# GpSimd fetches the scan's output and x of each unit by row index

## The chip, the cores and the metric

The kernel runs on one core of a Trainium2 chip. The metric is the device time of one execution in microseconds (us). TensorE (PE in the rows), VectorE (DVE), ScalarE (ACT) and GpSimd (POOL) compute; SyncE (SP) issues most of the transfers between device memory and the on-chip buffers. Every engine works through its own instructions in order and is held up by semaphores.

## What is computed

A block of a transformer on x of shape (4, 2048, 256), in float32:

```python
mod = (_silu(c) @ wmod)                       # sa, ca, ga, sb, cb, gb per batch
h = _layernorm(x) * (1 + ca) + sa
x = x + ga * attention(h)                     # a delta-rule layer, below
h = _layernorm(x) * (1 + cb) + sb
x = x + gb * experts(h)                       # 16 experts, 4 of them chosen, and a shared one

# attention(h): q, k, v from projections and short causal convolutions, then
delta = delta_rule_scan(q, k, v, beta)        # over chunks, in order of tokens
fs, fl = fir(v, 3 taps), fir(v, 31 taps)
stats = [mean and std per head of fs, fl, delta]
p = softmax(router([h, stats]))               # three weights for each head and token
o = p0 * fs + p1 * fl + p2 * delta + id_scale * v
o = o * rsqrt(mean(o * o) + 1e-5) * o_norm_w
return o @ Wo
```

## The kernel before

The kernel is a chain of stages, each a block of its own on all engines: `setup`, `norm_inputs`, `conv_heads`, `long_filter` (the 31 taps), `chunk_inverses`, `delta_scan`, and `mix_and_experts`. A stage ends with a barrier. The scan writes its output, delta, to device memory (`o_d`, 64 tiles of 128 tokens by 256); the last stage reads it back.

`mix_and_experts` starts some 1112 us into the span and works on 16 units of 512 tokens (`UT`; `J` = 4 tiles of 128 tokens). For each unit there are two pieces of work. The **mix** computes the statistics, the router, the mixture o, the projection with Wo, x + ga * (...), called `x2`, and the second layer norm. The **experts** part multiplies by 20 blocks of weights (4 of the shared expert, then 16 experts), `up` and `down` for each. `units_ahead` sets the order: the mix of unit 0 alone (`front`), then for each unit u a `body` that runs the experts of u and, threaded between its steps, the mix of u+1. The mix is cut into 40 small steps s, of which PE, ACT and DVE each take two after each of the 20 blocks. The loop over the bodies is rolled over the first three batches (four bodies in each turn), and the last four bodies are written out.

The inputs of a mix lie in two sets of buffers, by the parity of the unit: `vf` (v and the short filter), `fl` (the long filter), `dl` (delta), `xx` (x), `hT` (the normed h, transposed). SP loads them in `load(u, g, i)`, L1822 to L1836, eight transfers for a unit: one for `vf`, four for `fl`, one each for `dl`, `xx`, `hT`. SP waits first for `x2_done` of the unit two before, after which nothing reads the old content. All count on one semaphore for each parity, `loaded[i]`. Unit 0's `vf`, `fl` and `dl` are already on the chip, read for the scan stage, and SP loads only its `hT` and `xx`.

POOL's work in a body, in order of its queue (L1876 to L1911):
- `mix(u+1)`: two powers (L1880) that make the standard deviations for the statistics out of the variances that DVE has put into `mx_tmp`; then a product with `ids` (L1887), a product with the softmax weights (L1891), two more powers (L1894, L1896), each after a wait for DVE.
- `finish(u)`: after the last expert of unit u, the product with gb (L1903) and the sum with `x2` (L1906).

So the next instruction of POOL after `finish(u-1)` is the first power of `mix(u+1)` in body u. PE needs the result of both powers at step 8 of the mix, after block 4 of 20: there it waits for `std_done`, transposes the statistics (L1927) and goes on. All that PE has to do after this point, the `down` of block 4 first, stands behind that wait:

```python
if s == 8:
    pe.wait_ge(std_done, u * 2 + 2)
    pe.wait_ge(gexp_done, u + 1)
    for j in range(J):
        ins = pe.transpose(M[0][0:K3 * 2 * H, j * P:(j + 1) * P], st[:, j, :], m.ident[:])
```

DVE's `expert` step (L2316) weights each expert's `down` and adds it to `mx_acc`; it waits for PE.

In `chunk_inverses` POOL clears the semaphores of the early stages (L1118), 54 of them, between its first three loads and its first memset.

Of the kernel before, what the change touches and what calls it, by code (L numbers as in the profile page):

```python
# [10 lines left out]
P = 128  # L11
# [4 lines left out]
J = UT // P  # L16
UB = L // UT
NU = B * UB
# [211 lines left out]
def units_ahead(eng, front, body):  # L230

    front(0, 0)
    with eng.Fori(0, B - 1) as b:
        for g in range(UB):
            body(b * UB + g, g, b * UB + (g + 1))
    for g in range(UB):
        u = (B - 1) * UB + g
        body(u, g, u + 1 if g < UB - 1 else None)
# [502 lines left out]
def long_filter(nc, m, w):  # L741
# [10 lines left out]
    with ExitStack() as ctx:  # L752
# [3 lines left out]
        def sem(name):  # L756
            return ctx.enter_context(nc.semaphore(name))
# [12 lines left out]
        store = [sem(f"fl_store{i}") for i in range(RF)]  # L770
# [902 lines left out]
def mix_and_experts(nc, m, w):  # L1673
# [6 lines left out]
    with ExitStack() as ctx:  # L1680
        def sb(name, shape):
            return ctx.enter_context(nc.sbuf_tensor(name, shape, F32))

        def sem(name):
            return ctx.enter_context(nc.semaphore(name))
# [8 lines left out]
        vf = [m.vf0, m.kqT0[:].rearrange("p b a c -> p b (a c)")]  # L1694
        fl = [m.fl0, sb("mx_fl1", [P, J, D])]
# [99 lines left out]
        store = [sem(f"mx_store{i}") for i in two]  # L1795
        block = ctx.enter_context(nc.Block("mix_and_experts"))

        x_v = w.x.rearrange("b (g j p) d -> (b g) p j d", j=J, p=P)
        out_v = w.out.rearrange("b (g j p) d -> (b g) p j d", j=J, p=P)
# [9 lines left out]
        def _(sp):  # L1809
# [8 lines left out]
            sp.sem_inc(loaded[0], 96)  # L1818
# [5 lines left out]
            def load(u, g, i):  # L1824
                rows = bass.ds(u * J, J)

                sp.wait_ge(x2_done, u * 2 + 2)
                sp.dma_start(vf[i][:], m.vf_d[rows].rearrange("j p c -> p j c")).then_inc(loaded[i], 16)
                fl_b = m.fl_d[:, bass.ds(u // UB, 1)].squeeze(1)
                for j in range(J):  # L1830
                    first = (g * J + j) * P
                    sp.dma_start(fl[i][:, j, :].rearrange("p (y c) -> p y c", c=CF),
                                 fl_b[:, first:first + P, :].rearrange("y p c -> p y c")).then_inc(loaded[i], 16)
                sp.dma_start(dl[i][:], m.o_d[rows].rearrange("j p c -> p j c")).then_inc(loaded[i], 16)
                sp.dma_start(xx[i][:], x_v[bass.ds(u, 1)].squeeze(0)).then_inc(loaded[i], 16)
                sp.dma_start(hT[i][:], m.hT_d[bass.ds(u, 1)].squeeze(0)).then_inc(loaded[i], 16)  # L1836

            sp.dma_start(hT[0][:], m.hT_d[0]).then_inc(loaded[0], 16)
            sp.dma_start(xx[0][:], x_v[0]).then_inc(loaded[0], 16)
# [23 lines left out]
        def _(pool):  # L1863
            n = 0
            pool.memset(gsel[:], 1.0).then_inc(const_done, 1)
# [7 lines left out]
            def mix(u, i):  # L1873
# [10 lines left out]
                if isinstance(u, int) and u == 0:  # L1884
                    pool.wait_ge(loaded[i], (u - i) * 64 + 128)
# [10 lines left out]
                pool.tensor_tensor(rstd[:], mv[:, :, 1], m.half_pow[:, 0:J], ALU.pow).then_inc(rstd_done, 1)  # L1896

# [13 lines left out]
            def body(u, g, nxt):  # L1911
                if nxt is not None:
                    mix(nxt, (g + 1) % 2)
                finish(u, g % 2)

            units_ahead(pool, front, body)

        @block.tensor
        def _(pe):
            def mix(u, i, s):  # L1920
# [8 lines left out]
                if 8 <= s < 12:  # L1929
                    f = s - 8  # L1930
                    if f == 0:
                        pe.wait_ge(loaded[i], (u - i) * 64 + 128)
# [181 lines left out]
        def _(dve):  # L2114
            def mix(u, i, s):
                if s < 2:
# [3 lines left out]
                    if s == 0:  # L2120
                        dve.wait_ge(loaded[i], (u - i) * 64 + 128)
# [230 lines left out]
def build(nc, x, Wq, Wk, Wv, Wb, conv_q, conv_k, conv_v, fir_short, fir_long, alpha_id, Wid, bid, Wr1, br1,  # L2352
# [28 lines left out]
    with ExitStack() as ctx:  # L2381
        def sb(name, shape):
            return ctx.enter_context(nc.sbuf_tensor(name, shape, F32))
        m.ident = sb("ident", [P, P])
# [23 lines left out]
        m.ck = sb("ck", [P, NT * H])  # L2408
        mid = ctx.enter_context(ExitStack())
# [63 lines left out]
```

## Time and profile before

| | |
|---|---|
| median of 2 runs | 2588.45 us (2582.2 to 2594.7) |
| the profiled execution: its span | 2587.5 us |
| PE busy | 2394.4 us, 93% of the span |
| DVE busy | 1655.0 us, 64% |
| ACT busy | 1109.5 us, 43% |
| POOL busy | 616.3 us, 24% |
| mean granted clock of PE | 0.946 of full speed |

A profile row gives an instruction's line, engine and operation, what it writes and reads, how long it took, and how long its engine had been idle before it and for whom it waited. The idle time of an engine that waits for something later in the program costs nothing by itself; what counts is the chain of work that ends last. In the last stage that chain runs through PE's matmuls, with short pieces of DVE and POOL.

### The profile page before, as it was taken

How to read it: one execution, taken by the hardware profiler on the slowest of the kernel's cores; microseconds unless marked ns; L12 is line 12 of the kernel's file. 1: busy time of each engine (PE TensorE's matmuls, PEld its weight loads, DVE VectorE, ACT ScalarE, POOL GpSimd, SP SyncE). 2: the span in 40 equal slices, each digit the busy share in tenths (PEclk: the TensorE clock that was granted, in tenths of full speed). 3: DMA queues.
4: the chain of work that ended last, by engine and by line, in shares of the span. 5: the costliest groups of instructions: out<-in, count | busy, mean ns of one | idle time of the engine just before them, and what ended most of it. 6: DMA issues, size and time to landing. Idle time of an engine off the chain costs nothing.

```text
span 2587.5 us, 41994 instructions
## 1 busy us (share of the span) xinstructions
PE 2394.4 (93%) x14594; PEld 1659.7 (64%) x14594; DVE 1655.0 (64%) x4354; ACT 1109.5 (43%) x2350; POOL 616.3 (24%) x417
## 2 busy tenths in 40 slices
PE   6899997667897999979999999999999999999998
PEld 4466665555676888845666666666666666666665
DVE  4487886449922566525767676667667676766675
ACT  2477876346663222224334424433443344244331
POOL 1145554031101111211312231222123132312210
PEclk9999998787667999989999999999999999999999
DMA  5447556978767767421202210220122022101000
GB/s 166 162 149 219 174 166 192 270 212 203 212 155 223 217 204 225 156 74 49 58 1 58 58 50 9 58 58 13 45 59 58 1 58 58 43 15 58 9 9 8
DMA packets 376312, 272.14 MB, mean 105 GB/s; under 512 B 199714, under 2 KB 333794, under 8 KB 373906
## 3 DMA queue, kind: packets, MB, share of 16 engines
q1 hardware_dynamic: 371474, 243.85, 33.6%
q0 software_dynamic: 4640, 25.73, 2.9%
q8 instruction: 115, 1.88, 0.3%
q14 instruction: 83, 0.68, 0.1%
HBM read 168.60 MB, written 100.93 MB: 104 GB/s over the span
## 4 chain that ended last, share of the span: by engine, by line
PE 43%; DVE 9%; issue 3%; POOL 2%; ACT 0%; DMA 0%; DVEq 0%; SPq 0%; POOLq 0%; ACTq 0%
PE mx_dn L2002 16%; PE mx_up L1988 15%; PE mx_m L1938 4%; DVE mx_acc L2316 4%; PE mx_m L1965 2%; POOL mx_rms L1894 2%; PE mx_m L1942 1%; PE mx_m L1979 1%; DVE hl L2224 1%; DVE mx_st L2214 1%; DVE hl L2199 1%; DVE hl L2188 1%; DVE mx_rms L2193 1%; PE mx_m L1973 1%; PE mx_m L1947 1%
## 5 line engine op out<-in xcount | busy, mean ns | idle before, releaser
L2316 DVE SCALAR_TENSOR_TENSOR mx_acc<-mx_dn,mx_comb,mx_acc 128x256 f32<-128x256 f32 x1024 | 424.3, 478 | 356.6 <-PE mx_dn L2002 352.7
L2002 PE MATMUL mx_dn<-mx_edn,mx_hs 128*128 128x256 f32 x2048 | 487.7, 381 | 0.0
L1988 PE MATMUL mx_up<-mx_h2T,mx_eup 128*128 128x512 f32 x1024 | 484.3, 595 | 0.0
L2002 PEld LDWEIGHTS mx_dn<-mx_edn,mx_hs 128*128 128x128 f32 x2048 | 384.4, 190 | 145.6 <-issue 91.0
L2090 ACT ACTIVATE mx_hs<-mx_up 128x512 f32<-128x512 f32 x320 | 190.8, 596 | 625.8 <-PE mx_up L1988 625.1
L1988 PEld LDWEIGHTS mx_up<-mx_h2T,mx_eup 128*128 128x128 f32 x1024 | 190.9, 190 | 156.1 <-issue 145.2
L675 DVE SCALAR_TENSOR_TENSOR cv_acc<-cv_pre,conv_w,cv_acc 128x512 f32<-128x512 f32 x288 | 215.7, 750 | 78.2 <-ACT cv_acc L597 71.3
L539 PE MATMUL cv_pj<-cv_hT,wqkv 128*128 128x512 f32 x384 | 181.8, 604 | 12.7 <-ACT cv_acc L597 7.7
L713 POOL TENSOR_TENSOR rn<-cv_ss,half_pow 128x8 f32 x64 | 127.5, 1992 | 13.2 <-POOL cv_ss L709 13.2
L1880 POOL TENSOR_TENSOR mx_st<-mx_tmp,root_pow 128x24 f32<-128x24 f32 x30 | 124.6, 4168 | 20.1 <-DVE mx_tmp L2142 20.1
L1938 PE MATMUL mx_m<-mx_hT,wr 128*128 128x512 f32 x256 | 122.2, 601 | 3.3 <-DMA mx_x<-_attn_hidden_states_dram 2.5
L1653 ACT ACTIVATE ds_U<-ds_ups 64x256 f32<-64x256 f32 x64 | 24.1, 377 | 232.2 <-PE ds_ups L1517 232.2
L2002 PEld LDWEIGHTS mx_dn<-mx_sdn,mx_hs 128*128 128x128 f32 x512 | 97.3, 190 | 40.5 <-issue 30.6
L1988 PE MATMUL mx_up<-mx_h2T,mx_sup 128*128 128x512 f32 x256 | 120.7, 605 | 2.0 <-issue 2.0
L2002 PE MATMUL mx_dn<-mx_sdn,mx_hs 128*128 128x256 f32 x512 | 121.0, 379 | 0.0
L539 PEld LDWEIGHTS cv_pj<-cv_hT,wqkv 128*128 128x128 f32 x384 | 67.6, 192 | 73.2 <-issue 54.7
L1150 PE MATMUL ci_gps<-ci_kT 64*128 64x128 f32 x768 | 84.8, 361 | 20.5 <-ACT ci_A L1229 13.2
L1575 DVE TENSOR_TENSOR ds_att<-ds_attps,upper 128x256 f32<-128x256 f32 x128 | 48.4, 420 | 84.5 <-PE ds_attps L1495 82.6
L2090 ACT ACT_TABLE_LOAD x76 | 97.5, 1283 | 7.0 <-issue 3.3
L555 PE MATMUL cv_vfps<-diag_fs,cv_vT 128*128 128x128 f32 x768 | 97.4, 277 | 0.0
L817 PE MATMUL fl_ps<-fl_toep,fl_vc 128*84 128x98 f32 x512 | 51.9, 266 | 44.9 <-DVE fl_vc L861 20.6
L555 PEld LDWEIGHTS cv_vfps<-diag_fs,cv_vT 128*128 128x128 f32 x768 | 91.9, 194 | 0.0
(292 smaller groups left out, 3998.7 us busy)
## 6 DMA issues: line engine op xcount, KB each, us to landing
kqT_d<-cv_kqc SPq DMA_DIRECT2D x16, 1024.0 KB, 8.5
vf_d<-cv_vf SPq DMA_DIRECT2D x16, 1024.0 KB, 5.4
fl_toep<-taps_d SPq DMA_DIRECT2D x32, 392.0 KB, 7.3
ds_kqT<-kqT_d SPq DMA_DIRECT2D x10, 1024.0 KB, 5.9
fl_v<-vf_d SPq DMA_DIRECT2D x8, 1216.0 KB
ci_kT<-kqT_d POOLq DMA_DIRECT2D x19, 512.0 KB, 5.7
fl_d<-fl_out POOLq DMA_DIRECT2D x8, 1029.0 KB, 7.2
xin<-_attn_hidden_states_dram SPq DMA_DIRECT2D x16, 512.0 KB, 4.3
```

The costliest lines, as they stand in the source:

```text
L539: ins = pe.matmul(pj[o % 2][:], m.wqkv[:, k, weight(o) * P:(weight(o) + 1) * P], hT[i][:, k, :], start=(k == 0), stop=(k == KD - 1))
L555: ins = pe.matmul(vf_ps[j % 2][:, D + k * P:D + (k + 1) * P], vT[i][:, k, c0 + t:c0 + t + P], m.diag_fs[:, k, t, :], start=(t == 0), stop= ...
L675: ins = dve.scalar_tensor_tensor(out=acc[o % 3][:], in0=pre[i][:, o, t:t + UT], scalar=m.conv_w[:, weight(o), t:t + 1], in1=acc[o % 3][:], ...
L713: pool.tensor_tensor(m.rn[:, bass.ds(u * (J * 2 * H) + j * 2 * H, 2 * H)], ss[j % 2][:], m.half_pow[:, 0:2 * H], ALU.pow).then_inc(rn_done, 1)
L817: ins = pe.matmul(ps[g % RP][0:NA, c // 4, (c % 4) * WIN:(c % 4 + 1) * WIN], vc[:, g % GH * TC + c, :], m.toep[g % RT][:, c, ::-1], start= ...
L1150: ins = pe.matmul(g_ps[n % 2][h % 2][:, h // 2 * P:(h // 2 + 1) * P], kT[k % KB][r, b, h // 2, :], kT[k % KB][r, b, h // 2, :], start=True ...
L1880: pool.tensor_tensor(std[:, :, 1, :], tmp[:, 2, part].rearrange("p (a h) -> p a h", h=H), m.root_pow[:, part].rearrange("p (a h) -> p a h" ...
L1938: pe.matmul(M[(f + 1) % 2][:], m.wr1[:, k, f * P:(f + 1) * P], hT[i][:, k, :], start=(k == 0), stop=False)
L1988: ins = pe.matmul(up_ps[x % 2][:], lhs, h2T[i][:, k, :], start=(k == 0), stop=(k == KD - 1))
L2002: ins = pe.matmul(dn_ps[(i + n) % 2][:, j, :], hs[x % 4][:, j * P:(j + 1) * P], rhs, start=(x == 0 and j % 2 == 0) or x >= NS, stop=(x >= ...
L2090: act.activation(hs[x % 4][:], up_ps[x % 2][:], ACT.Silu).then_inc(silu_done, 1)
L2316: ins = dve.scalar_tensor_tensor(out=acc[i][:, j, :], in0=dn_ps[(i + n) % 2][:, j, :], scalar=comb[i][:, j, e:e + 1], in1=acc[i][:, j, :], ...
```

## The change

`dl` and `xx` are no longer loaded by SP. POOL makes a table of row numbers once (an iota of 128 x 64, `mx_rows_i`). A new function `fetch(u, i)` copies the four columns of unit u into `rows_u[i]`, waits for its own copy and for `x2_done`, and issues eight indirect transfers: for each of the four tiles one of 128 rows of `o_d` into `dl` and one of 128 rows of x into `xx`, 128 KB each. `fetch(0)` and `fetch(1)` stand ahead of the mix of unit 0; `fetch(u+2)` stands at the start of body u, for u = 0 to 13. The transfers count on new semaphores `rows_in[i]`, for which DVE waits at the start of each mix beside `loaded[i]`, whose counts fall by 32 for each unit. The new semaphores and two older sets are allocated once for the whole kernel instead of within a stage, and the semaphores of `long_filter` join the list that POOL clears in `chunk_inverses`.

```diff
@@ long_filter
-        store = [sem(f"fl_store{i}") for i in range(RF)]
+        store = m.fl_store
+        m.early_sems += [*v_in, mm_done, act_turned, dve_turned, *ev_done, m.v_zero, m.v_first, *m.toep_in]
@@ mix_and_experts
+        rows_i = ctx.enter_context(nc.sbuf_tensor("mx_rows_i", [P, NT], mybir.dt.int32))
+        rows_u = [ctx.enter_context(nc.sbuf_tensor(f"mx_rows_u{i}", [P, J], mybir.dt.int32)) for i in two]
...
+        x_rows = w.x.rearrange("b l d -> (b l) d")
+        o_rows = m.o_d.rearrange("n p d -> (n p) d")
@@ sync
-            sp.sem_inc(loaded[0], 96)
+            sp.sem_inc(loaded[0], 80)
...
-                sp.dma_start(dl[i][:], m.o_d[rows].rearrange("j p c -> p j c")).then_inc(loaded[i], 16)
-                sp.dma_start(xx[i][:], x_v[bass.ds(u, 1)].squeeze(0)).then_inc(loaded[i], 16)
                 sp.dma_start(hT[i][:], m.hT_d[bass.ds(u, 1)].squeeze(0)).then_inc(loaded[i], 16)
 
             sp.dma_start(hT[0][:], m.hT_d[0]).then_inc(loaded[0], 16)
-            sp.dma_start(xx[0][:], x_v[0]).then_inc(loaded[0], 16)
@@ gpsimd
+            pool.iota(rows_i[:], [[P, NT]], base=0, channel_multiplier=1).then_inc(iota_done, 1)
+            pool.wait_ge(iota_done, 1)
...
+            def fetch(u, i):
+
+                pool.tensor_copy(rows_u[i][:], rows_i[:, bass.ds(u * J, J)]).then_inc(rows_done, 1)
+                pool.wait_ge(rows_done, u + 1)
+                pool.wait_ge(x2_done, u * 2 + 2)
+                pool.sem_inc(fetch_go, 1)
+                for j in range(J):
+                    pool.indirect_dma_start(dl[i][:, j, :], None, o_rows, bass.IndirectOffsetOnAxis(rows_u[i][:, j:j + 1], 0))\
+                        .then_inc(rows_in[i], 16)
+                    pool.indirect_dma_start(xx[i][:, j, :], None, x_rows, bass.IndirectOffsetOnAxis(rows_u[i][:, j:j + 1], 0))\
+                        .then_inc(rows_in[i], 16)
+
...
             def body(u, g, nxt):
+                if not isinstance(u, int) or u + 2 < NU:
+                    fetch(u + 2, g % 2)
                 if nxt is not None:
                     mix(nxt, (g + 1) % 2)
                 finish(u, g % 2)
 
+            fetch(0, 0)
+            fetch(1, 1)
             units_ahead(pool, front, body)
@@ tensor, and alike on gpsimd and vector
-                        pe.wait_ge(loaded[i], (u - i) * 64 + 128)
+                        pe.wait_ge(loaded[i], (u - i) * 48 + 96)
@@ vector, first step of a mix
+                        dve.wait_ge(rows_in[i], (u - i) * 64 + 128)
```

On POOL, between the body of one unit and the next within the rolled loop, the queue of the kernel before reads thus; the two rows that write `mx_acc` are `finish(u-1)`, and the rows that write `mx_st` are the two powers at the head of the next mix (an ISA row is a semaphore step or a register load).

```order
L1903 TENSOR_TENSOR mx_acc<-mx_acc,gbB 128x1024
L1906 TENSOR_TENSOR mx_acc<-mx_acc,mx_x 128x1024
L1878 ISA
L1880 TENSOR_TENSOR mx_st<-mx_tmp,root_pow 128x6x4
L1878 REGISTER_ALU
L1880 TENSOR_TENSOR mx_st<-mx_tmp,root_pow 128x6x4
L1887 TENSOR_TENSOR kv<-kqT,mx_ids 128x1024
```

At the same place the queue of the changed kernel reads as follows; `mx_rows_u` holds the row numbers, and three more pairs of the two DMA rows follow where the dots stand, before the powers.

```order
L1920 TENSOR_TENSOR mx_acc<-mx_acc,gbB 128x1024
L1923 TENSOR_TENSOR mx_acc<-mx_acc,mx_x 128x1024
L1905 ISA
L1905 COPY mx_rows_u<-mx_rows_i 128x4
L1906 REGISTER_ALU
L1907 ISA
L1910 DMA mx_dl<-o_d,mx_rows_u 128x256
L1912 DMA mx_x<-in_L_attn_hidden_states_dram,mx_rows_u 128x256
...
L1883 REGISTER_ALU
L1885 TENSOR_TENSOR mx_st<-mx_tmp,root_pow 128x6x4 x2
L1892 TENSOR_TENSOR kv<-kqT,mx_ids 128x1024
```

A copy, a semaphore step and eight transfers now stand between the sum with `x2` and the two powers; nothing else on POOL has moved in the bodies.

On SP, the start of the rolled loop's body in the kernel before, from the last transfer of `fl` on:

```order
L1832 DMA mx_fl<-fl_d 128x8x32
L1834 ISA
L1834 DMA mx_dl<-o_d 128x4x256
L1835 ISA
L1835 DMA mx_x<-in_L_attn_hidden_states_dram 128x4x256
L1836 DMA mx_hT<-hT_d 128x1024
L1843 REGISTER_ALU
L1844 ISA
L1844 DMA out_dram<-mx_acc 128x4x256
```

and the same place in the changed kernel:

```order
L1838 DMA mx_fl<-fl_d 128x8x32
L1840 ISA
L1840 DMA mx_hT<-hT_d 128x1024
L1846 REGISTER_ALU
L1847 ISA
L1847 DMA out_dram<-mx_acc 128x4x256
```

The two direct transfers of 512 KB have left SP's queue, and `hT` and the store of the unit's result have moved up by them.

## Rows read from the trace of the kernel before

**Rows 1.** The page: busy us, share of the span and instructions of each engine

```profile
PE 2394.4 (93%) x14594; PEld 1659.7 (64%) x14594; DVE 1655.0 (64%) x4354; ACT 1109.5 (43%) x2350; POOL 616.3 (24%) x417
```

**Rows 2.** Timeline of POOL at one body's start: start, us, instruction, [idle before <-releaser]

```profile
1445.51 2.36 POOL L1903 TENSOR_TENSOR mx_acc<-mx_acc,gbB 128x1024 f32<-128x1024 f32 x1 [12.00 <-DVE mx_acc L2316]
1447.94 2.34 POOL L1906 TENSOR_TENSOR mx_acc<-mx_acc,mx_x 128x1024 f32<-128x1024 f32 x1
1451.16 8.31 POOL L1880 TENSOR_TENSOR mx_st<-mx_tmp,root_pow 128x24 f32<-128x24 f32 x2 [0.88 <-DVE mx_tmp L2142]
```

**Rows 3.** Timeline of PE around step 8, in the body before and in this

```profile
1371.72 0.60 PE L1927 MATMUL mx_m<-ident,mx_st 128*24 128x128 f32 x4
...
1458.82 1.88 PE L1988 MATMUL mx_up<-mx_h2T,mx_eup 128*128 128x512 f32 x4
1460.54 0.60 PE L1927 MATMUL mx_m<-ident,mx_st 128*24 128x128 f32 x4
1460.97 1.88 PE L1938 MATMUL mx_m<-mx_hT,wr 128*128 128x512 f32 x4
```

**Rows 4.** Timeline of DVE in the same body, the first experts' sums

```profile
1466.56 1.66 DVE L2316 SCALAR_TENSOR_TENSOR mx_acc<-mx_dn,mx_comb,mx_acc 128x256 f32<-128x256 f32 x4 [0.21 <-DVE mx_comb L2300]
...
1472.85 1.66 DVE L2316 SCALAR_TENSOR_TENSOR mx_acc<-mx_dn,mx_comb,mx_acc 128x256 f32<-128x256 f32 x4 [4.34 <-PE mx_dn L2002]
1479.26 1.66 DVE L2316 SCALAR_TENSOR_TENSOR mx_acc<-mx_dn,mx_comb,mx_acc 128x256 f32<-128x256 f32 x4 [4.75 <-PE mx_dn L2002]
```

**Rows 5.** Timelines of POOL and PE in the next body, which opens a loop turn

```profile
1536.76 2.35 POOL L1906 TENSOR_TENSOR mx_acc<-mx_acc,mx_x 128x1024 f32<-128x1024 f32 x1
1541.53 8.30 POOL L1880 TENSOR_TENSOR mx_st<-mx_tmp,root_pow 128x24 f32<-128x24 f32 x2 [2.43 <-DVE mx_tmp L2142]
...
1550.63 0.60 PE L1927 MATMUL mx_m<-ident,mx_st 128*24 128x128 f32 x4
```

**Rows 6.** POOL's instructions grouped: xcount | busy us, mean ns | idle before

```profile
L709 POOL TENSOR_TENSOR cv_ss<-cv_ss,l_eps 128x8 f32<-128x8 f32 x64 | 39.1, 611 | 140.9 <-DVE cv_ss L684 140.9
...
L1896 POOL TENSOR_TENSOR mx_rstd<-mx_mv,half_pow 128x4 f32<-128x4 f32 x16 | 16.1, 1006 | 191.1 <-DVE mx_mv L2220 191.1
...
L1096 POOL DMA_DIRECT2D ci_kT<-kqT_d x19 | 14.3, 755 | 57.7 <-PE ci_gps L1150 50.6 <-POOLq L752 7.0
```

**Rows 7.** The instructions of one line: POOL's stores of `fl_d` (duration ns min/median/max)

```profile
L784 POOL DMA_DIRECT2D fl_d<-fl_out x8: 513/513/755, 461.7 to 536.2; - x8
```

**Rows 8.** Timeline of POOL in `chunk_inverses`: a transfer and the memset behind it

```profile
556.95 0.76 POOL L1096 DMA_DIRECT2D ci_kT<-kqT_d  x1
557.70 0.97 POOL L1124 MEMSET ci_half<- 128x1024 f32 x1
```

**Rows 9.** The instructions of one line: the semaphores cleared there, first and last start

```profile
L1118 POOLq EVENT_SEMAPHORE_RANGE_CLEAR  x54: 44/44/48, 544.5 to 548.3; - x54
```

**Rows 10.** Timelines of PE at the start of the last stage (mix of unit 0)

```profile
1115.78 2.07 PE L2010 MATMUL mx_dn<-wr,ident 128*128 128x512 f32 x2 [4.75 <-DVE mx_pick L2346]
...
1121.20 5.56 PE L1938 MATMUL mx_m<-mx_hT,wr 128*128 128x512 f32 x8 [2.50 <-DMA mx_x<-_attn_hidden_states_dram]
...
1128.59 3.70 PE L1938 MATMUL mx_m<-mx_hT,wr 128*128 128x512 f32 x8 [0.77 <-ACT mx_hm L2054]
```

**Rows 11.** Stretches: us, busy of five engines, granted clock, DMA share, GB/s

```profile
1115.00:1120.00 5.00, 2.93 (x6) 1.07 (x6) 0.23 (x1) 1.23 (x3) 1.25 (x4) 0.50 0.54 169
1120.00:1125.00 5.00, 3.80 (x5) 1.73 (x6) 0.35 (x2) 1.23 (x1) 1.90 (x1) 0.50 0.99 290
1125.00:1130.00 5.00, 4.23 (x12) 1.45 (x12) 0.00 (x0) 1.27 (x2) 0.00 (x0) 1.00 0.83 199
...
1460.00:1480.00 20.00, 20.00 (x65) 10.58 (x64) 10.39 (x24) 12.80 (x15) 1.90 (x1) 1.00 0.22 75
```

**Rows 12.** Timelines of POOL and DVE in the mix of unit 0

```profile
1116.27 0.52 POOL L1870 TENSOR_SCALAR_AFFINE_SELECT mx_esel<-mx_esel 128x256 f32<-128x256 f32 x1
1121.79 1.90 POOL L1887 TENSOR_TENSOR kv<-mx_vf,mx_ids 128x1024 f32<-128x1024 f32 x1 [5.01 <-DVE mx_ids L2149]
1140.91 2.96 POOL L1891 TENSOR_TENSOR kv<-mx_vf,mx_pr 128x1024 f32<-128x1024 f32 x1 [17.21 <-DVE mx_pr L2172]
...
1166.88 1.01 POOL L1896 TENSOR_TENSOR mx_rstd<-mx_mv,half_pow 128x4 f32<-128x4 f32 x1 [12.62 <-DVE mx_mv L2220]
...
1138.88 0.21 DVE L2153 TENSOR_TENSOR mx_pr<-mx_m,rtau 128x48 f32<-128x48 f32 x1 [17.24 <-PE mx_m L1952]
...
1146.24 1.22 DVE L2188 TENSOR_TENSOR hl<-hl,kv 128x1024 f32<-128x1024 f32 x1
```

**Rows 13.** Timeline of PE at step 8 of the mix of unit 1

```profile
1194.08 0.60 PE L1927 MATMUL mx_m<-ident,mx_st 128*24 128x128 f32 x4
```

**Rows 14.** DMA issues: xcount, KB each, median us from issue to landing

```profile
mx_dl<-o_d SPq DMA_DIRECT2D x16, 512.0 KB, 4.5
...
mx_x<-_attn_hidden_states_dram SPq DMA_DIRECT2D x16, 512.0 KB, 5.2
```

More of the change, by code:

```diff
@@ L1794, in mix_and_experts @@
         last_step = sem("mx_last_step")
-        store = [sem(f"mx_store{i}") for i in two]
+        store = m.mx_store
+        iota_done, rows_done, fetch_go, rows_in = m.iota_done, m.rows_done, m.fetch_go, m.rows_in
         block = ctx.enter_context(nc.Block("mix_and_experts"))
         x_v = w.x.rearrange("b (g j p) d -> (b g) p j d", j=J, p=P)
+        x_rows = w.x.rearrange("b l d -> (b l) d")
+        o_rows = m.o_d.rearrange("n p d -> (n p) d")
         out_v = w.out.rearrange("b (g j p) d -> (b g) p j d", j=J, p=P)
@@ L1884, in mix @@
                 if isinstance(u, int) and u == 0:
-                    pool.wait_ge(loaded[i], (u - i) * 64 + 128)
+                    pool.wait_ge(loaded[i], (u - i) * 48 + 96)
                 pool.wait_ge(ids_step, u * 2 + 2)
@@ L2120, in mix @@
                     if s == 0:
-                        dve.wait_ge(loaded[i], (u - i) * 64 + 128)
+                        dve.wait_ge(loaded[i], (u - i) * 48 + 96)
+                        dve.wait_ge(rows_in[i], (u - i) * 64 + 128)
                     if isinstance(u, int) and u == 0:
@@ L2383, in sb @@
             return ctx.enter_context(nc.sbuf_tensor(name, shape, F32))
+        m.mx_store = [ctx.enter_context(nc.semaphore(f"mx_store{i}")) for i in range(2)]
+        m.iota_done = ctx.enter_context(nc.semaphore("mx_iota_done"))
+        m.rows_done = ctx.enter_context(nc.semaphore("mx_rows_done"))
+        m.fetch_go = ctx.enter_context(nc.semaphore("mx_fetch_go"))
+        m.rows_in = [ctx.enter_context(nc.semaphore(f"mx_rows_in{i}")) for i in range(2)]
         m.ident = sb("ident", [P, P])
@@ L2408, in build @@
         m.ck = sb("ck", [P, NT * H])
+        m.fl_store = [ctx.enter_context(nc.semaphore(f"fl_store{i}")) for i in range(3)]
         mid = ctx.enter_context(ExitStack())
```

## Prediction

> **What bounds the kernel now.** I read the busy shares first [rows 1]: PE works 93% of the span, POOL 24%, so PE sets the pace and POOL has room on average. An average says nothing of a deadline inside a unit, so next come the timelines of one body. Each body of the last stage takes 88.8 us (PE's step 8 at 1371.72 and at 1460.54 [rows 3]; 90.1 to the next at 1550.63, which opens a turn of the loop [rows 5]). Within it the reader is to follow POOL from the end of one unit to the start of the next [rows 2]: the sum with x2 ends at 1447.94 + 2.34 = 1450.28, the first power starts 0.88 later, when DVE's variances are there, and the two powers end at 1451.16 + 8.31 = 1459.47. PE starts the transposes that need them at 1460.54 with no idle time shown [rows 3]. So POOL meets PE's deadline by 1460.54 - 1459.47 = 1.07 us, and all that may be put ahead of the powers at no cost is 0.88 + 1.07 = 1.95 us. Where a loop turn opens, the same sum is 1550.63 - (1536.76 + 2.35) - 8.30 = 3.22 us [rows 5].
>
> What if PE is late there? DVE after this point waits for PE: 4.34 and 4.75 us before the second and third expert's sum [rows 4]. It hurries nothing and makes up nothing; its work moves later with PE's. A delay of PE at step 8 is a delay of the unit, whole. PE's clock is also at stake: the stretch around this point is granted 1.00 [rows 11].
>
> **The change, part by part.**
>
> *Eight indirect transfers and a copy ahead of the powers, in bodies 0 to 13.* The trace before has no indirect transfer. POOL's direct ones occupy it: 0.513 us for a store of 84 long rows [rows 7], 0.755 for a load in 512 pieces of 1 KB [rows 6], and the memset behind one starts when it ends, 556.95 + 0.76 against 557.70 [rows 8]. Issuing is thus work that POOL does in line. An indirect transfer of 128 rows writes 128 pieces of 1 KB, so its lower bound is the direct price, 0.51. On top POOL must read 128 row numbers from the chip's buffer. The cheapest of POOL's small operations that read a tile is 0.61 us (L709, 128 x 8), one of the index table's own width 1.01 (L1896, 128 x 4, a power) [rows 6]. The upper bound is 0.755 + 1.01 = 1.76. I take 0.51 + 0.61 = 1.12, because an index read is nearer to a plain read than to a power. Eight are 9.0 us. The copy of 128 x 4 and its two waits: nothing at the least, 0.7 at the most (0.61 by L709 and a semaphore step), I take 0.5. Together 9.5 us a body (bounds 4.4 and 14.8).
>
> The Trainium skill has a rule on this in "DMA: Bandwidth & Descriptors", section "Anatomy of one DMA — SWDGE (gpsimd) path": the fixed 2 us of such a transfer is mostly completion, and generating descriptors is a small, variable part of which one can emit a lot before it shows. The rows agree for direct ones (some 430 pieces more cost 0.24 us); by that rule the sum would be the lower bound's. No row here shows it with an index read.
>
> What stands behind: the two powers on POOL, then PE's transposes, PE's `down` of block 4, and with it DVE and ACT. Delay a body: 9.5 - 1.95 = 7.55 us, and 9.5 - 3.22 = 6.28 where a loop turn opens. Of the 14 bodies, body 0 has more room: POOL is free at 1166.88 + 1.01 = 1167.89 [rows 12] and PE's step 8 is at 1194.08 [rows 13], so 26.19 - 8.30 = 17.9 us are free, and nothing is lost. Of bodies 1 to 13, two (4 and 8) open a loop turn. Sum: 11 x 7.55 + 2 x 6.28 = 95.6 us. Bounds: 11 x 2.45 + 2 x 1.18 = 29 and 11 x 12.85 + 2 x 11.58 = 165.
>
> *PE's clock after such a stall.* At the start of this stage PE idles for 4.75 us, and the granted clock is 0.50, the lower of its two levels (1.2 of 2.4 GHz), over the next 10 us, then 1.00 again [rows 10, 11]. Eight matmuls of L1938 took 5.56 us there and 3.70 after it; the two before took 2.07 instead of 2 x 3.70/8 = 0.93 [rows 10]. Lost: 1.86 + 1.14 = 3.0 us. A stall of 7.5 us a body is longer than that idle time, so I count 3.0 for each of 13: 39 us. Bounds: 0, if the clock stays, and half of ten, 5.1, if the whole 10 us are filled: 0 to 66.
>
> *The transfers themselves.* They land after some 5 us [rows 14], and DVE first needs them a body later, about 88.8 us; even several times that is covered. DVE's new wait for `rows_in` therefore costs nothing in the bodies, and the 16 direct transfers of each array that it replaces were as well covered.
>
> *The mix of unit 0.* Here POOL has to issue 16 transfers ahead of its product L1887. POOL's constants end at 1116.79 [rows 12]; with the iota, no longer than the select of 0.52 there, at 1117.3. `fetch(0)` ends at 1126.8 and lands at 1132.0 with the 5.2 of [rows 14]; DVE waits there, but first has other than the two small `ids` steps to do at 1138.88 [rows 12]: covered. `fetch(1)` ends at 1136.3, L1887 at 1138.2, before L1891 can start at 1140.91: covered. At 1.76 each, `fetch(1)` would end at 1146.9, L1887 and L1891 (1.90 + 2.96) at 1151.8, and DVE's sum that wants them at 1146.24 would be 5.5 late; that is the upper bound. PE gains a little: it waited 2.50 us for x [rows 10], which SP no longer loads; PE now waits for `hT` alone, issued just before. Between 0 and 2.5; I take 0.5.
>
> *22 more semaphores cleared.* 54 took from 544.5 to 548.3 [rows 9], 70 ns each; 22 more are 1.5 us on POOL ahead of its first memset and further loads of `ci_kT`. At worst it comes through whole: +1.5; at best nothing. I take 1.5.
>
> *SP.* Two transfers fewer for each unit; nobody waits for SP's queue in the bodies. Zero.
>
> Sum: 95.6 + 39 - 0.5 + 1.5 = 135.6. On the profiled execution's own span of 2587.5 us that gives 2723 us; the median of the runs, 2588.45, is the same within 0.1%.
>
> **The rivals.**
>
> *Cheap issue: no change to speak of.* POOL writes the 128 pieces almost as fast as a direct transfer, 0.55 us each, and the short stall leaves the clock alone. Then a body has 4.8 us of fetch, the stall is 2.85 us (1.6 at a loop turn), together 35 us: 2587.5 + 35 + 1 = 2623 us. For it: 0.513 in [rows 7]. Against it: the row numbers have to be read, and PE's clock fell after 4.75 us. It holds up to 0.7 us a transfer (13 stalls and 1 us more then come to 2%), and only if the clock stays; if the clock falls each time, 39 us of the 52 are gone, and only a fetch of 3.1 us would do. 0.12.
>
> *Dearer issue, 1.9 to 4 us a transfer.* POOL would wait within each transfer for something that no row shows. At 3 us: fetch 24.5, delay 22.5 x 11 + 21.3 x 2 = 290, clock 39, body 0 late by 6.6, unit 0's mix by some 26 (49 from 1117.3, then 4.86, against 1146.24): 2587.5 + 362 = 2950 us. 0.10.
>
> *POOL becomes the bound.* If each row number is fetched by itself, one after the other, at 611/8 = 76 ns (L709's price for a column [rows 6]), a transfer takes 9.8 us, a fetch 78.7. Delay: 11 x 76.7 + 2 x 75.5 = 995, 133 in unit 0's mix (two fetches from 1117.3 to 1274.7, then 4.86), 61 in body 0, 45 of clock and the rest: 3820 us. For it: no row shows POOL reading one number per partition to address memory. Against it: POOL's 512 pieces in 0.755 us are 1.5 ns each, far from 76. The Trainium skill states such a price in "GPSIMD Engine Reference", section "7. Performance pitfalls for Q7 kernels": about 102 cycles for every small read command, one per gather index, that doesn't overlap the one before; at its 1.2 GHz that is 85 ns, and by it alone the time would be some 3960 us (an estimate). No run here shows it. 0.06.
>
> *Faster.* All that could be gained is PE's 2.50 us at the start of the stage. 0.02 for anything beyond 2%.
>
> **How the numbers follow.** Two per cent is 52 us, about what a measurement of this kernel can tell from no change. My forecast, a transfer of 0.7 to 1.9 us with the clock falling, has 0.70: its bounds are 2587.5 + 29 + 39 at the low end (2655) and 165 + 66 + 5.5 + 1.5 at the high one (2825). The cheap rival (0.12) ends as "same", the two dear ones (0.10, 0.06) as slower, so slower is 0.86, same 0.12, faster 0.02. To leave out no more than 2 in 10 the range goes from 2640, which reaches into the cheap rival's upper end, to 2830; outside remain most of the cheap rival and the dear ones.
>
> **What would show it.** In the profile of the changed kernel: the mean of POOL's DMA rows at L1910 and L1912 (1.1 us forecast); POOL's idle time before L1885 gone, because the powers now start when the fetch ends; PE idle before the transposes of `mx_st` (now L1948) with POOL's L1885 as releaser, 7.5 us in 13 bodies and none in body 0; the granted clock at 0.50 right behind; body length up from 88.8 to about 99.3 us; no wait of DVE for `rows_in` but in unit 0. I am wrong if PE does not wait at L1948, if the DMA rows are under 0.7 us, or if DVE's or PE's time moves elsewhere, for instance by transfers that land later than a body after their issue.

## The result, and the profile after

The changed kernel takes 2748.11 us (2748.07 to 2748.16, 2 runs) against 2588.45 us: a ratio of 1.062, with a 95% interval of 1.056 to 1.068. The profiled execution has a span of 2746.4 us, 158.9 us more than the one before. The forecast was 2723 us, within 2640 to 2830.

The page of the changed kernel, busy time of each engine and, from its fourth part, the chain of work that ended last by engine:

```profile
PE 2435.5 (89%) x14594; PEld 1682.2 (61%) x14594; DVE 1657.0 (60%) x4354; ACT 1111.3 (40%) x2350; POOL 755.6 (28%) x562
...
PE 33%; POOL 11%; DVE 9%; issue 5%; ACT 0%; DVEq 0%; DMA 0%; POOLq 0%; SPq 0%; ACTq 0%
```

The same chain in the kernel before:

```profile
PE 43%; DVE 9%; issue 3%; POOL 2%; ACT 0%; DMA 0%; DVEq 0%; SPq 0%; POOLq 0%; ACTq 0%
```

PE has the same 14594 matmuls as in [rows 1]. POOL has 139 us more of work and is still idle for 72% of the span, but its share of the chain went from 2% to 11%. An engine with ample room on average now sets the end in places. The view of PE's waits says where (waited for, us in total, times, longest):

```profile
PE mx_m L1948 <- POOL mx_st L1885: 127.1, 13, 11.3
```

In the kernel before this wait has no row at all. It is step 8 of the mix, PE waiting for the two powers, 13 times. POOL's timeline at the start of one body shows what stands ahead of them; it answers to [rows 2]:

```profile
1376.81 2.35 POOL L1923 TENSOR_TENSOR mx_acc<-mx_acc,mx_x 128x1024 f32<-128x1024 f32 x1
1379.11 0.18 POOL L1905 COPY mx_rows_u<-mx_rows_i 128x4 int32 x1
1380.19 1.07 POOL L1910 DMA_INDIRECT mx_dl<-o_d,mx_rows_u  x1 [0.90 <-POOL mx_rows_u L1905]
1381.56 0.95 POOL L1912 DMA_INDIRECT mx_x<-_attn_hidden_states_dram,mx_rows_u  x1 [0.30 <-issue]
...
1386.56 1.00 POOL L1912 DMA_INDIRECT mx_x<-_attn_hidden_states_dram,mx_rows_u  x1 [0.30 <-issue]
1387.86 1.68 POOL L1910 DMA_INDIRECT mx_dl<-o_d,mx_rows_u  x1 [0.30 <-issue]
1389.84 0.95 POOL L1912 DMA_INDIRECT mx_x<-_attn_hidden_states_dram,mx_rows_u  x1 [0.30 <-issue]
1390.81 8.51 POOL L1885 TENSOR_TENSOR mx_st<-mx_tmp,root_pow 128x24 f32<-128x24 f32 x2
```

From the end of the sum with x2 (1376.81 + 2.35 = 1379.16) to the first power (1390.81) it is 11.65 us, where there was 0.88 before. Most of the transfers take 0.95 us (the first takes 1.07, the seventh 1.68), and 0.30 us of idle time follows each: 1.25 us from start to start. PE at the same place, against [rows 3]:

```profile
1387.68 1.88 PE L2009 MATMUL mx_up<-mx_h2T,mx_eup 128*128 128x512 f32 x4
1399.45 1.02 PE L1948 MATMUL mx_m<-ident,mx_st 128*24 128x128 f32 x4 [9.88 <-POOL mx_st L1885]
1400.26 2.88 PE L1959 MATMUL mx_m<-mx_hT,wr 128*128 128x512 f32 x4
1402.98 1.89 PE L2023 MATMUL mx_dn<-mx_edn,mx_hs 128*128 128x256 f32 x8
```

PE idles for 9.88 us, and then its first matmuls are slow: 1.02 us for what took 0.60, 2.88 for 1.88. The same stretch cut in windows (us, busy of five engines, granted clock, DMA share, GB/s), against [rows 11]:

```profile
1390.00:1392.00 2.00, 0.00 (x0) 0.00 (x0) 1.97 (x2) 1.11 (x2) 1.98 (x2) 1.00 1.15 308
1392.00:1402.00 10.00, 2.55 (x7) 1.32 (x8) 3.03 (x10) 1.46 (x3) 7.32 (x2) 0.50 0.11 39
1402.00:1412.00 10.00, 10.00 (x32) 5.30 (x31) 1.91 (x6) 5.26 (x6) 1.90 (x1) 0.99 0.01 2
```

The clock falls to its lower level while PE idles, and stays there for some 10 us; PE works for 2.55 of these. DVE makes up nothing. Its timeline behind the stall, against [rows 4]:

```profile
1404.90 1.66 DVE L2338 SCALAR_TENSOR_TENSOR mx_acc<-mx_dn,mx_comb,mx_acc 128x256 f32<-128x256 f32 x4 [9.67 <-PE mx_dn L2023]
...
1413.13 1.66 DVE L2338 SCALAR_TENSOR_TENSOR mx_acc<-mx_dn,mx_comb,mx_acc 128x256 f32<-128x256 f32 x4 [6.28 <-PE mx_dn L2023]
1419.54 1.66 DVE L2338 SCALAR_TENSOR_TENSOR mx_acc<-mx_dn,mx_comb,mx_acc 128x256 f32<-128x256 f32 x4 [4.75 <-PE mx_dn L2023]
```

It waited 0.21 us for `mx_comb` before the first sum and now waits 9.67 us for PE; the third waits 4.75 as before.

Because a run's span also holds what happens in the six earlier stages, the experiments are compared by a distance inside the last stage: from the start of PE's step-8 transposes of unit 1 to that of unit 15, each read from PE's timeline. That is 14 bodies with all 13 stalls. Before, it is 1245.8 us (14 x 88.8 and a little at the loop turns). "Rest" is what the distance has grown by, less the wait.

| kernel | unit 1 to unit 15, us | over before | PE's wait for POOL in it | rest | rest for each of 13 stalls |
|---|---|---|---|---|---|
| after | 1399.7 | 153.9 | 127.1 | 26.8 | 2.1 |
| after, once more (e8) | 1401.9 | 156.1 | 127.5 | 28.6 | 2.2 |
| SP loads, rest kept (e3) | 1245.9 | 0.1 | 0 | 0.1 | |
| fetch behind the powers (e1) | 1247.2 | 1.4 | 0 | 1.4 | |
| x only (e2) | 1329.7 | 83.9 | 57.0 | 26.9 | 2.1 |
| direct on POOL (e4) | 1324.5 | 78.6 | 55.5 | 23.1 | 1.8 |
| sixteen of 64 rows (e7) | 1522.9 | 277.0 | 246.8 | 30.2 | 2.2 (of 14) |
| ten matmuls added (e6) | 1376.8 | 131.0 | 15.8 | 115.2 | 0.1 beside the 8.75 added |
| twenty matmuls added (e5) | 1485.4 | 239.5 | 0 | 239.5 | less than the 17.33 added |

In e7 PE also waits in body 0; that wait lies ahead of the distance, but what follows it lies within, so its rest is shared by 14 stalls.

Of the 158.9 us, 127.1 are PE's waits and 26.8 the rest; the last 5.0 lie outside this distance.

### The profile page after: what moved, and what is told of

Read it like the earlier page. It is cut to its first block, busy times and chain, and to the rows that moved or that the text cites. A ratio compares the mean times of both kernels' runs of the same rounds, so it can differ in the third digit from the quotient of the medians.

```text
span 2746.4 us, 42140 instructions
## 1 busy us (share of the span) xinstructions
PE 2435.5 (89%) x14594; PEld 1682.2 (61%) x14594; DVE 1657.0 (60%) x4354; ACT 1111.3 (40%) x2350; POOL 755.6 (28%) x562
## 3 DMA queue, kind: packets, MB, share of 16 engines
q8 instruction: 115, 1.88, 0.3%
## 4 chain that ended last, share of the span: by engine, by line
PE 33%; POOL 11%; DVE 9%; issue 5%; ACT 0%; DVEq 0%; DMA 0%; POOLq 0%; SPq 0%; ACTq 0%
PE mx_dn L2023 12%; PE mx_up L2009 9%; DVE mx_acc L2338 5%; PE mx_m L1959 5%; POOL mx_st L1885 4%; POOL mx_dl L1910 2%; PE mx_m L1986 2%; POOL mx_x L1912 2%; POOL mx_rms L1899 2%; PE mx_m L1963 1%; POOL mx_acc L1920 1%; PE mx_m L2000 1%; DVE hl L2246 1%; DVE mx_st L2236 1%; DVE hl L2221 1%
## 5 line engine op out<-in xcount | busy, mean ns | idle before, releaser
L2009 PEld LDWEIGHTS mx_up<-mx_h2T,mx_eup 128*128 128x128 f32 x1024 | 190.9, 190 | 156.1 <-issue 145.2
L1959 PE MATMUL mx_m<-mx_hT,wr 128*128 128x512 f32 x256 | 140.1, 677 | 1.7 <-DMA mx_hT<-hT_d 1.0
L713 POOL TENSOR_TENSOR rn<-cv_ss,half_pow 128x8 f32 x64 | 127.5, 1991 | 13.2 <-POOL cv_ss L709 13.2
L1948 PE MATMUL mx_m<-ident,mx_st 128*24 128x128 f32 x64 | 15.6, 395 | 127.1 <-POOL mx_st L1885 127.1
L1885 POOL TENSOR_TENSOR mx_st<-mx_tmp,root_pow 128x24 f32<-128x24 f32 x30 | 127.6, 4261 | 1.2 <-DVE mx_tmp L2164 0.9
L2075 ACT ACTIVATE mx_hm<-mx_m,br 128x512 f32<-128x512 f32 x64 | 43.8, 687 | 133.6 <-PE mx_m L1963 133.2
```

The costliest lines, as they stand in the source:

```text
L713: pool.tensor_tensor(m.rn[:, bass.ds(u * (J * 2 * H) + j * 2 * H, 2 * H)], ss[j % 2][:], m.half_pow[:, 0:2 * H], ALU.pow).then_inc(rn_done, 1)
L1885: pool.tensor_tensor(std[:, :, 1, :], tmp[:, 2, part].rearrange("p (a h) -> p a h", h=H), m.root_pow[:, part].rearrange("p (a h) -> p a h" ...
L1959: pe.matmul(M[(f + 1) % 2][:], m.wr1[:, k, f * P:(f + 1) * P], hT[i][:, k, :], start=(k == 0), stop=False)
L2009: ins = pe.matmul(up_ps[x % 2][:], lhs, h2T[i][:, k, :], start=(k == 0), stop=(k == KD - 1))
```

## The experiments

**Does anything but the transfers cost time?** SP loads both arrays again, while the table, the copy with its wait, the new semaphores and the longer clearing list stay. Left out below are the counts of `loaded`, which go back to the old ones, SP's load of unit 0's x, and DVE's wait for `rows_in`, which goes.

```diff
@@ sync, load
+                sp.dma_start(dl[i][:], m.o_d[rows].rearrange("j p c -> p j c")).then_inc(loaded[i], 16)
+                sp.dma_start(xx[i][:], x_v[bass.ds(u, 1)].squeeze(0)).then_inc(loaded[i], 16)
@@ gpsimd, fetch
-                for j in range(J):
-                    pool.indirect_dma_start(dl[i][:, j, :], None, o_rows, bass.IndirectOffsetOnAxis(rows_u[i][:, j:j + 1], 0))\
-                        .then_inc(rows_in[i], 16)
-                    pool.indirect_dma_start(xx[i][:, j, :], None, x_rows, bass.IndirectOffsetOnAxis(rows_u[i][:, j:j + 1], 0))\
-                        .then_inc(rows_in[i], 16)
```

> No indirect transfer is left: SP loads both arrays directly; POOL still makes its table, copies the columns of each unit, waits and counts, and the semaphores are allocated and cleared as in the changed kernel. Theory A: 0.2 to 1.2 us a body fit into the 1.95 us of room, nothing waits; 2594 us if the later start of the last stage (5.3 us in the profile) comes from the bookkeeping of the semaphores, 2588 us if that was chance.

It took 2584.67 us (2581.05 to 2594.99, 10 runs), ratio 0.998 (0.996 to 1.001), and its bodies are those of before (0.1 us over all of them). So no cost of POOL's bookkeeping shows, nor one of the longer list of semaphores; the interval would hide no more than some 1 us.

**Is it the transfers, or their place?** The same eight transfers, put behind the two powers instead of ahead of them.

```diff
-            def mix(u, i):
+            def mix(u, i, then=None):
@@ mix, behind the second power
+                if then is not None:
+                    then()
@@ body
-                if not isinstance(u, int) or u + 2 < NU:
-                    fetch(u + 2, g % 2)
+                more = not isinstance(u, int) or u + 2 < NU
                 if nxt is not None:
-                    mix(nxt, (g + 1) % 2)
+                    mix(nxt, (g + 1) % 2, (lambda: fetch(u + 2, g % 2)) if more else None)
```

> The eight indirect transfers of each body stay on POOL, but stand behind the two powers instead of ahead of them. Theory A (what costs is the place: the fetch delays the powers, and PE waits for them at step 8): PE's wait at L1948 is gone, the clock stays, the product with ids comes some 2.5 us later on POOL, where it has 20 us to spare; 2594 us, that is before plus the 5 to 6 us by which the last stage already began later in the profile of the changed kernel. Rival B (the indirect transfers cost as such: by their number, by contention for buffers or memory, or by landing late): it stays above 2700 us.

It took 2591.68 us (2586.71 to 2607.7, 10 runs), ratio 1.0025 (1.0002 to 1.0048). POOL's timeline of one body in this kernel:

```profile
1368.50 8.30 POOL L1885 TENSOR_TENSOR mx_st<-mx_tmp,root_pow 128x24 f32<-128x24 f32 x2 [0.88 <-DVE mx_tmp L2165]
1376.75 0.47 POOL L1907 COPY mx_rows_u<-mx_rows_i 128x4 int32 x1
1378.10 1.14 POOL L1912 DMA_INDIRECT mx_dl<-o_d,mx_rows_u  x1 [0.89 <-POOL mx_rows_u L1907]
1379.55 0.95 POOL L1914 DMA_INDIRECT mx_x<-_attn_hidden_states_dram,mx_rows_u  x1 [0.30 <-issue]
...
1387.99 1.92 POOL L1894 TENSOR_TENSOR kv<-kqT,mx_ids 128x1024 f32<-128x1024 f32 x1
```

The copy and the transfers cost POOL about what they did, 11.2 us of a body (1376.75 to 1387.99) against 11.65, and the powers have their 0.88 us back. PE has no wait for them. So the loss is the place in POOL's queue: all of it but some 3 us goes when the fetch stands behind two instructions instead of ahead of them. GpSimd can fetch these rows at next to no cost; it only may not do so ahead of the powers.

**Half the transfers.** POOL fetches x, SP loads delta; the counts that follow from it are left out below.

```diff
@@ sync, load
+                sp.dma_start(dl[i][:], m.o_d[rows].rearrange("j p c -> p j c")).then_inc(loaded[i], 16)
@@ gpsimd, fetch
-                    pool.indirect_dma_start(dl[i][:, j, :], None, o_rows, bass.IndirectOffsetOnAxis(rows_u[i][:, j:j + 1], 0))\
-                        .then_inc(rows_in[i], 16)
```

> POOL fetches x alone (four indirect transfers a body, at the old place); SP loads the scan's output directly as before the change. Theory A: the fetch falls from 11.65 us to 1.07 + 4 x 1.25 = 6.1 us, PE's wait at step 8 from 9.8 to about 4.3 us, the clock still falls in each body (2.4 us): 13 x 6.7 = 87 us and 5 us from the stages ahead, 2680 us. If the price were mostly fixed for a body (the copy, its waits, the clock), it would stay above 2720 us; if the clock fell only behind long stalls, 2650 us.

It took 2668.74 us (2663.7 to 2678.41, 4 runs), ratio 1.034 (1.030 to 1.037). PE's waits:

```profile
PE mx_m L1947 <- POOL mx_st L1886: 57.0, 13, 4.6
```

Four transfers fewer take 70.1 us from the waits, 5.4 for each body: four times 1.25, and the one long transfer, which this kernel doesn't have, less what its powers take more. The price of the fetch grows with the number of transfers. The rest stays at 2.1 us for each stall, though the stall is less than half as long.

**What does the row index cost?** The same eight transfers of 128 rows, in the same place, as direct ones without an index tile; `x_t` is x seen as tiles of 128 rows.

```diff
-                    pool.indirect_dma_start(dl[i][:, j, :], None, o_rows, bass.IndirectOffsetOnAxis(rows_u[i][:, j:j + 1], 0))\
-                        .then_inc(rows_in[i], 16)
-                    pool.indirect_dma_start(xx[i][:, j, :], None, x_rows, bass.IndirectOffsetOnAxis(rows_u[i][:, j:j + 1], 0))\
-                        .then_inc(rows_in[i], 16)
+                    pool.dma_start(dl[i][:, j, :], m.o_d[bass.ds(u * J + j, 1)].squeeze(0)).then_inc(rows_in[i], 16)
+                    pool.dma_start(xx[i][:, j, :], x_t[bass.ds(u * J + j, 1)].squeeze(0)).then_inc(rows_in[i], 16)
```

> POOL issues eight direct transfers of 128 rows at the place of the eight indirect ones, of the same rows and sizes; the table and the copy stay. If reading the row numbers is what makes an indirect transfer dearer than the 0.51 us of a direct one (0.95 us busy was measured), a transfer falls to 0.51 us busy plus 0.30 between two, the fetch to some 8.3 us, the delay to 6.3: 13 x 8.7 = 113 us over 2590, 2703 us. If writing 128 pieces costs the same either way, 2748 us.

It took 2664.57 us (2651.09 to 2679.56, 4 runs), ratio 1.028 (1.023 to 1.033), some 40 us less than expected. POOL's timeline, and PE's row behind it:

```profile
1384.46 0.54 POOL L1912 DMA_DIRECT2D mx_x<-_attn_hidden_states_dram  x1
1385.01 9.39 POOL L1886 TENSOR_TENSOR mx_st<-mx_tmp,root_pow 128x24 f32<-128x24 f32 x2
...
1394.53 1.03 PE L1947 MATMUL mx_m<-ident,mx_st 128*24 128x128 f32 x4 [4.49 <-POOL mx_st L1886]
```

Direct transfers follow one another at 0.54 us without a gap, near the 0.51 of [rows 7]; indirect ones at 1.25. The index tile therefore makes a transfer 0.71 us dearer, and eight are 5.7 us. With the one long transfer of each body gone (0.7 more), PE's wait should fall by 6.4; it fell by 5.4 in this body, since the powers now take 9.39 us instead of 8.51 (more on that below).

**By the transfer or by the row?** Sixteen indirect transfers of 64 rows in place of eight of 128.

```diff
-            pool.iota(rows_i[:], [[P, NT]], base=0, channel_multiplier=1).then_inc(iota_done, 1)
+            pool.iota(rows_i[:], [[64, 2 * NT]], base=0, channel_multiplier=1).then_inc(iota_done, 1)
...
-                for j in range(J):
-                    pool.indirect_dma_start(dl[i][:, j, :], None, o_rows, bass.IndirectOffsetOnAxis(rows_u[i][:, j:j + 1], 0))\
+                for j in range(2 * J):
+                    r = slice(j % 2 * 64, j % 2 * 64 + 64)
+                    pool.indirect_dma_start(dl[i][r, j // 2, :], None, o_rows, bass.IndirectOffsetOnAxis(rows_u[i][0:64, j:j + 1], 0))\
...
```

> The same rows in sixteen indirect transfers of 64 rows a body in place of eight of 128. If an indirect transfer's price is mostly fixed, each stays near 0.95 us busy plus 0.30: the fetch is 21.9 us, 13 x 22.3 us of delay and clock, and the mix of unit 0 starts some 18 us late: about 2900 us. If it is mostly by the row, each falls to some 0.5 us, the fetch is 14.3 us: about 2785 us.

It took 2886.09 us (2881.49 to 2894.16, 4 runs), ratio 1.116 (1.111 to 1.120), near the number for a fixed price. The instructions of the line that fetches delta (duration ns min/median/max), first of this kernel, then of the changed one:

```profile
L1911 POOL DMA_INDIRECT mx_dl<-o_d,mx_rows_u x128: 902/907/1667, 1118.9 to 2636.8; - x128
```

```profile
L1910 POOL DMA_INDIRECT mx_dl<-o_d,mx_rows_u x64: 942/946/1696, 1123.6 to 2497.0; - x64
```

Half the rows take 0.04 us from the median, with the same 0.30 us gap behind. The price is per transfer. The row numbers are not paid for one by one: 64 of them cost 0.04 us, where the rival that forecast 3820 us wanted 76 ns each. The Trainium skill's "GPSIMD Engine Reference", section "7. Performance pitfalls for Q7 kernels", puts a price of about 102 cycles on each of many small read commands, such as one for each index; the trace does not agree for this instruction, and the measurement decides.

This kernel also shows where the cover of body 0 ends. PE's wait for the powers comes 14 times, once more than elsewhere, and the additional one is 5.2 us, in body 0: a fetch there lasts 21.5 us (16 x 1.21, 1.08 for the copy, and a long one), and the room, 17.9 us in the prediction, is 16.4 here (POOL is free at 1185.02, and without its wait PE would be there at 1209.75; the powers take 8.34).

**Is the rest the clock?** If PE works ahead of step 8 instead of idling, the wait is filled and the clock should stay. Twenty matmuls whose result nobody reads are added there, in every body.

```diff
                 if s == 8:
-                    pe.wait_ge(std_done, u * 2 + 2)
                     pe.wait_ge(gexp_done, u + 1)
+                    if not isinstance(u, int) or u > 0:
+                        for y in range(20):
+                            pe.matmul(M[0][:], m.ident[:], m.wr1[:, y % KD, :], start=True, stop=True)
+                    pe.wait_ge(std_done, u * 2 + 2)
```

> The changed kernel with twenty matmuls of 128 x 512 that nothing reads (9.3 us at the full clock) put on PE ahead of its wait at step 8 in each body, so that PE is busy while POOL fetches. If the clock's fall behind the stall costs what the profile seems to show (each body is some 12 us longer, but PE's wait is 9.8), the granted clock stays at 1.00 and the time falls by 13 x 2.4 = 31 us to 2717 us. If those 2.4 us are something else, it stays at 2748 us or rises.

It took 2849.57 us (2846.23 to 2857.27, 4 runs), ratio 1.103 (1.099 to 1.107): a miss, and one of the filler's size. PE's timeline:

```profile
1411.95 17.33 PE L1948 MATMUL mx_m<-wr,ident 128*128 128x512 f32 x40
1429.11 0.60 PE L1951 MATMUL mx_m<-ident,mx_st 128*24 128x128 f32 x4
```

Each of the twenty stands as two matmuls, so that they take 17.33 us and not some 9; they outlast the wait, and PE waits no more for POOL. The transposes take 0.60 us again. But with the filler longer than the wait, the time alone can't tell how the clock counts, so the next run has ten at the same place, in the bodies up to the one that holds the mix of unit 14.

```diff
+                    if not isinstance(u, int) or 0 < u < NU - 1:
+                        for y in range(10):
+                            pe.matmul(M[0][:], m.ident[:], m.wr1[:, y % KD, :], start=True, stop=True)
```

> As the run with twenty unread matmuls on PE ahead of its wait at step 8, but with ten. Its trace showed each of them as two passes of 0.433 us, 17.3 us in place of the 9.3 counted, so they outlasted the fetch; ten are 8.7 us and end before the powers do (PE waited 9.8 us). If the clock's fall costs 2.4 us a body, 13 bodies give back 31 us and body 0, where PE did not wait, loses 8.7: 22 us less than the changed kernel, 2726 us. If the clock is not it, 2757 us.

It took 2735.95 us (2725.99 to 2738.18, 4 runs), ratio 1.056 (1.052 to 1.061). The changed kernel beside it on the same chip:

> The changed kernel unaltered, beside the next three on one chip. 2748 us, within 10 us to either side, since the kernel before scatters by that much from run to run.

2744.9 us (2742.56 to 2748.59, 4 runs), ratio 1.061 (1.057 to 1.065). PE does more work and ends 9 us earlier. That is less than expected, and the intervals of the two ratios overlap, so the bodies must decide. PE's timeline with ten matmuls added, and its granted clock there:

```profile
1396.65 8.75 PE L1948 MATMUL mx_m<-wr,ident 128*128 128x512 f32 x20
1406.62 0.61 PE L1951 MATMUL mx_m<-ident,mx_st 128*24 128x128 f32 x4 [1.23 <-POOL mx_st L1885]
1407.06 1.88 PE L1962 MATMUL mx_m<-mx_hT,wr 128*128 128x512 f32 x4
```

```profile
1405.00:1410.00 5.00, 3.77 (x15) 2.25 (x15) 0.00 (x0) 2.46 (x3) 1.56 (x1) 1.00 0.00 0
```

8.75 us of filler and 1.23 of wait hold PE as long as the 9.88 of the changed kernel did, the clock stays at 1.00 (it falls in one body only, behind a wait of 2.69 us), and most bodies take 98.8 us, where the changed kernel's take 100.1 to 102.7. In the table the rest falls from 2.1 us for a stall to 0.1. So the rest is the clock, and it is worth 2 us a stall.

## Why the prediction was right, and by how much its terms were off

**The place of the loss: right.** A room of 1.95 us in front of a deadline of PE; PE late by what the fetch exceeds it; the unit later, whole. The wait sits at L1948 with L1885 as releaser, in bodies 1 to 13 and not in body 0, and at the two loop turns it is 8.57 and 8.39 us instead of 9.88, lower by 1.3 to 1.5 where the prediction had 1.27. In body 12, the first that is written out, it is 11.31, which the prediction hadn't singled out. Moving the fetch by two places in the queue undoes it (e1).

**The price of a transfer: 1.12 forecast, 1.25 measured.** The busy part, 0.95, was too dear in the forecast and the gap of 0.30 behind it wasn't in it. The step was "0.51 + 0.61", the direct price and the cheapest small read; the direct price holds (0.54 in e4), and the index adds 0.71. The copy and its waits were put at 0.5; copy and wait take 0.18 + 0.90 = 1.08, since POOL idles until its own copy is signalled. And one transfer a body takes 1.41 to 1.96 us instead of 0.95. A fetch is then 11.65 us, not 9.5. Less 1.95 of room, plus the 0.20 us by which the powers got longer (8.51 against 8.31), that is the 9.88 us that PE waits. Term: 95.6 forecast, 127.1 measured. (The lower bound of 4.4 us for a fetch is eight times 0.55; with the 0.51 named there it is 4.1, and the term's lower bound 25 us instead of 29. The 26 us of the dearer rival in unit 0's mix come to 24.9. Neither moves the range.)

**The clock: 3.0 forecast, 2.1 measured for a stall.** The 3.0 came from the start of the stage [rows 10, 11], where PE works through most of its 10 slow us. Here the low clock begins within the stall, so part of it falls on time in which PE does nothing anyway: in the windows above PE works 2.55 of 10 us at 0.50, half of which, 1.3 us, is lost; that body is 100.2 us against the 98.8 with the clock kept. Of the other eleven bodies between two stalls four take 100.1 to 100.3 as well, the rest 100.9 to 102.7; in the one of 101.5 PE works 5.02 of the 10 us at 0.50 (1293 to 1303). Term: 39 forecast, 26.8 measured. The two errors have opposite signs, and their sum, 134.6 against 153.9, leaves 19.3 us that the forecast missed within the bodies; that the total came nearer than its largest term, which was 31.5 us short, is luck.

**What was put at nothing.** The bookkeeping on POOL: 0.1 us over all bodies (e3). Body 0: no wait. SP's shorter queue: nobody waited for it. DVE waits for a fetched row just once, in the mix of unit 0, as forecast (15.6 us, where it has little else to do); transfers land in 5.5 us at the median, a body ahead of need. Unit 0's mix: from its transposes to those of unit 1 it is 75.9 us, 76.4 before, and 68 to 76 in the profiles of e1 to e4 (e7, with twice the transfers, has 96.6), so no loss shows, and a gain as small as the 0.5 forecast can't be read. Within it one piece of work got slower: POOL's product L1892, now behind both fetches, runs beside DVE's L2191, which takes 1.87 us there and 0.21 in the other 15 mixes. PE's wait for x of 2.50 us [rows 10] is one of 1.0 for `hT`.

**The semaphores: 1.5 forecast, nothing found.** 76 clears now run where 54 did:

```profile
L1119 POOLq EVENT_SEMAPHORE_RANGE_CLEAR  x76: 37/38/47, 543.8 to 548.6; - x76
```

From the first start to the last it is 4.8 us where [rows 9] had 3.8, the last starts 0.3 us later, and e3, which has them all, is not slower. The 5.0 us outside the distance come from the start of the last stage, where POOL's first instruction is at 1120.99 instead of 1115.46. This start moves from run to run, from 1116 to 1135 us by the first transposes in these profiles, in no relation to the edits; runs of one kernel differ by some 20 us. Nothing here ties it to the change.

**The rivals.** "Cheap issue" (0.55 us a transfer, clock untouched, 2623 us) would have been near for direct transfers: e4 has that price, but the clock falls there too, behind 11 of its 13 waits (4.49 us in most bodies), and it takes 2665. "Dearer issue" falls with 1.25 us, "POOL becomes the bound" with e7, and nothing became faster. None of these kernels beats the one before; e1 comes within 0.5% of it.

## What to carry to other kernels

Before work is put on an engine that looks idle, find the next instruction behind it for which another engine waits, and the slack of that one; here it was 2 us in a body in which POOL worked a quarter of the time, and two places further down the queue there was room for all of it. An indirect transfer's price on POOL is by the transfer, so move many rows with each. And a stall of the matrix engine costs more than its length: add what the clock gives away behind it, about 2 us on average for stalls of 4 to 19 us here.

## What the runs showed of the hardware that was not expected

**An indirect transfer keeps POOL for 1.2 us or a little more, with 64 rows as with 128:** 0.95 busy and a gap of 0.30 for 128 rows of 1 KB, 0.91 and 0.30 for 64 rows, against 0.54 without a gap for a direct one.

**Beside some operations of DVE it takes longer, by a simple sum.** The one long transfer of each body is always one that starts while DVE is well inside one of its two comparisons (L2298, L2299), which read two operands from the on-chip buffer. DVE's rows beside the long transfer at 1387.86 above:

```profile
1387.49 1.23 DVE L2298 TENSOR_TENSOR mx_hm<-mx_ms 128x1024 f32<-128x1024 f32 x1
1388.64 1.22 DVE L2299 TENSOR_TENSOR mx_hm<-mx_ms 128x1024 f32<-128x1024 f32 x1
```

L2298 ends at 1388.72, 0.86 us after the transfer began; the transfer takes 1.68, which is 0.86 and another 0.82. In all 13 bodies the long transfer takes what was left of DVE's operation and 0.81 to 0.84 us more, though what was left varies from 0.60 to 1.14. In e2, whose fetch ends before the comparisons begin, no transfer takes more than 1.13 us; in e1, where all but the end of one lies ahead of the fetch, none takes more than 1.21. Transfers that start inside DVE's reciprocal (L2259, one operand, 0.30 us left) take 0.95. It looks as if the transfer can't begin its real work until the operation with two operands ends; what it waits for inside the chip is only argued. The powers that start beside such operations are longer too, 9.39 us in e4 against 8.31 alone. The Trainium skill has such a rule in "SBUF — State Buffer", section "SBUF: two separate sides": a GpSimd operation that reads the buffer and a VectorE operation with two inputs from it share one pair of ports; whichever starts first holds it for its whole instruction, and the other waits. The trace agrees where POOL comes second, as above, and where L2191 starts inside POOL's product (1.87 us instead of 0.21). It doesn't for the powers: DVE's L2305, with two operands, starts inside a power in 13 of its 16 executions and takes 1.22 or 1.23 us in all 16.

**The clock's loss hardly grows with the stall.** On average the rest is 1.8 (e4) and 2.1 us (e2) for waits of some 4.3 us, 2.1 for 9.8, 2.2 for 19 (e7). That the rest is the clock was tested for the waits of 9.8 alone. With the longest waits the clock is at 0.50 for 17 to 20 us of a body, but most of that falls into the stall itself. In e4 it stays at 1.00 behind the waits of 2.79 and 3.12 us, which is why the mean is lower there.

**A float32 matmul can stand as two in the trace:** the twenty added ones of 128 x 512 with a 128 x 128 operand are 40 rows of 0.43 us each.
